# Turning the rows of the experts two tiles ahead in a four-layer metaformer

## What is computed

```
x = x + mixer_l(norm(x))            # l = 0: fractal, 1: involution, 2: splines, 3: squared-cosine attention
t = t + experts_l(norm(t))          # l = 0..3
# experts_l, for each token and each of its K chosen experts e:
h = act(x @ W1[e] + b1[e])          # layer 0: relu, top 1 of 8, F = 512, capacity, nan_to_num
y = weight * (h @ W2[e] + b2[e])    # layers 1, 2: gelu, top 2 of 8, F = 512 and 256
# layer 3, no biases: y = weight * ((silu(x @ W1[e]) * (x @ W2[e])) @ W3[e]), top 2 of 16, F = 256
```

## Time and profile before

| | |
|---|---|
| median of 3 runs | 2163.42 us (2162.23 to 2166.87) |
| profiled execution | 2167.0 us |
| its span, first to last instruction | 2165.2 us |
| mean granted clock of TensorE | 0.907 of full speed |
| TensorE, VectorE busy | 81%, 72% |

### The profile page before, as it was taken

One profiled execution on the slowest core, in us unless ns is written; L12 is line 12 of the kernel. 1 busy time (PEld: TensorE's weight loads), 2 busy tenths in 40 slices (PEclk: granted clock), 3 DMA queues, 4 the chain that ended last, 5 costly groups with the idle time before them and its releaser, 6 DMA issues. The chain is left out here.

```text
span 2165.2 us, 44747 instructions
## 1 busy us (share of the span) xinstructions
PE 1762.2 (81%) x10980; PEld 1383.6 (64%) x10981; DVE 1550.7 (72%) x4814; ACT 1200.6 (55%) x2719; POOL 957.5 (44%) x959
## 2 busy tenths in 40 slices
PE   2687666898588888899896776788859999979996
PEld 2233666897343434799895444667647777778996
DVE  8998887679677777655787576645866677665575
ACT  5455776798333323677685333556655444455664
POOL 0000234444105243675652277777630354557765
PEclk9999666999699999999998787798979999999998
DMA  3002002232201020132531112235422010124365
GB/s 81 0 0 78 18 24 61 60 94 84 87 5 36 22 61 29 56 97 77 151 102 50 56 51 80 70 99 155 138 77 98 20 37 31 54 54 105 100 196 157
DMA packets 183595, 154.30 MB, mean 71 GB/s; under 512 B 40294, under 2 KB 162822, under 8 KB 183362
## 3 DMA queue, kind: packets, MB, share of 16 engines
q1 hardware_dynamic: 153410, 92.37, 16.1%
q0 software_dynamic: 29952, 59.26, 8.1%
HBM read 85.33 MB, written 68.79 MB: 71 GB/s over the span
## 5 line engine op out<-in xcount | busy, mean ns | idle before, releaser
L1756 POOL DMA_INDIRECT returned<-rows_second_choice x488 | 495.9, 1016 | 310.2 <-DVE rows_second_choice L1677 107.4
L1307 POOL DMA_INDIRECT dispatched<-rows_first_choice,slot x192 | 191.9, 999 | 493.7 <-DVE rows_second_choice L1203 441.6
L1536 PE MATMUL psum<-rows_first_choice 128*128 128x128 f32 x2816 | 382.7, 280 | 19.4 <-DVE rows_first_choice L1658 19.2
L1536 PEld LDWEIGHTS psum<-rows_first_choice 128*128 128x128 f32 x2816 | 349.5, 195 | 24.5 <-DVE rows_first_choice L1658 23.5
L1546 PE MATMUL psum<-expert_weights,rows_first_choice 128*128 x2240 | 323.9, 283 | 24.6 <-DVE rows_second_choice L1674 11.0
L1546 PEld LDWEIGHTS psum<-expert_weights,rows_first_choice 128*128 128x128 f32 x2240 | 282.8, 195 | 37.5 <-issue 33.1
L1606 ACT ACTIVATE rows_first_choice<-psum,bias_columns 128x128 f32<-128x128 f32 x832 | 238.4, 375 | 91.3 <-PE psum L1536 89.2
L1307 POOL DMA_INDIRECT dispatched<-rows_second_choice,slot x192 | 187.9, 979 | 58.5 <-issue 58.2
L1307 POOL DMA_INDIRECT dispatched<-rows_first_choice,expert_weights x64 | 61.8, 966 | 266.7 <-DVE rows_first_choice L1201 249.4
L1589 ACT ACTIVATE rows_first_choice<-expert_weights 128x512 f32 x216 | 136.8, 634 | 44.0 <-issue 43.6
L1528 PE MATMUL psum<-identity,rows_second_choice 128*128 128x128 f32 x488 | 137.6, 283 | 14.1 <-DMA rows_second_choice<-dispatched 14.0
(11 more groups left out here) (423 smaller groups left out, 3834.1 us busy)
## 6 DMA issues: line engine op xcount, KB each, us to landing
rows_second_choice<-dispatched SPq DMA_DIRECT2D x488, 65.0 KB
rows_second_choice<-returned SPq DMA_DIRECT2D x10, 1024.0 KB, 6.0
returned<-rows_second_choice POOLq DMA_INDIRECT x488
expert_weights<-in_L_ffn_w SPq DMA_DIRECT2D x3, 2048.0 KB, 8.3
expert_weights<-returned SPq DMA_DIRECT2D x6, 1024.0 KB, 5.6
channel_major<-returned SPq DMA_DIRECT2D x6, 1024.0 KB, 7.1
residual<-in_x SPq DMA_DIRECT2D x8, 512.0 KB, 7.3
rows_second_choice<-returned SPq DMA_DIRECT2D x8, 512.0 KB, 4.4
```

The costliest lines, as they stand in the source:

```text
L1307: pool.indirect_dma_start(out=self.k.dispatched, out_offset=bass.IndirectOffsetOnAxis(ap=self.slot[:, b % 2, c, t:t + 1], axis=0), in_=sel ...
L1536: ins = pe.matmul(k.ps[:, self.PSH + u % 2, j * P:(j + 1) * P], self.wc[:, u % 2, j * P:(j + 1) * P], self.xt[:, u % 2, :], start=True, st ...
L1756: pool.indirect_dma_start(out=k.returned[0:N * self.K, :], out_offset=bass.IndirectOffsetOnAxis(ap=self.rt[:, u, C:C + 1].bitcast(I32), ax ...
```

## The change

Rows are turned two tiles ahead: in step t TensorE turns tile t+2 and VectorE copies tile t+2. Two turns and two copies stand ahead of the first step instead of one. The turned rows have four places instead of two. A turn now also waits until the copy of the tile two before it has read the PSUM bank. copy_rows waits in all layers until the hidden of four tiles before has read the place. The weight copies of VectorE raise `w_copied`, as ScalarE's did already, and hidden waits for it in all layers. Two more places of 128 columns shift rooms of the next norm in layer 2 by 256 columns.

```diff
-            rooms = [k.wts[:, 8192:8192 + 2 * IMG], rows1[:, late:late + 2 * IMG], rows0[:, 3840:3840 + 2 * IMG]]
-            slots = [rows0[:, 5888:5888 + IMG], rows0[:, 5888 + IMG:5888 + 2 * IMG], k.ch[:, N:N + IMG]]
+            rooms = [k.wts[:, 8192:8192 + 2 * IMG], rows1[:, late:late + 2 * IMG], rows0[:, 4096:4096 + 2 * IMG]]
+            slots = [rows0[:, 6144:6144 + IMG], rows0[:, 6144 + IMG:6144 + 2 * IMG], k.ch[:, N:N + IMG]]
...
-        self.xt, self.wc, self.hs = room(0, 2, C), room(0, 2, wide), room(0, self.HB, F)
+        self.xt, self.wc, self.hs = room(0, 4, C), room(0, 2, wide), room(0, self.HB, F)
...
         def turn_rows(t, u):
             pe.wait_ge(s_row[u].h, s_row[u].base + (t - u) * (16 // RING) + 16)
+            if past(t, 2):
+                pe.wait_ge(*self.when("x_copied", t - 1))
...
         def hidden(t, u):
             pe.wait_ge(*self.when("x_copied", t + 1))
-            if not self.vector_copies:
-                pe.wait_ge(*self.when("w_copied", t + 1))
+            pe.wait_ge(*self.when("w_copied", t + 1))
...
-                                self.xt[:, u % 2, :], start=True, stop=True)
+                                self.xt[:, u % 4, :], start=True, stop=True)
...
         def step(t, u, last):
             at = t if isinstance(t, int) else -1
-            if not last:
-                turn_rows(t + 1, (u + 1) % RING)
+            if not isinstance(t, int) or t + 2 < self.T:
+                turn_rows(t + 2, (u + 2) % RING)
...
         turn_rows(0, 0)
+        turn_rows(1, 1)
...
-            dve.tensor_copy(self.wc[:, u % 2, :], self.first[:, bass.ds(e, 1), :].rearrange("p a f -> p (a f)"))
+            dve.tensor_copy(self.wc[:, u % 2, :],
+                            self.first[:, bass.ds(e, 1), :].rearrange("p a f -> p (a f)")).then_inc(self.s["w_copied"].h, 1)
 
         def copy_rows(t, u):
             dve.wait_ge(*self.when("x_turned", t + 1))
-            if past(t, 2) and not self.vector_copies:
-                dve.wait_ge(*self.when("hidden_ready", t - 1))
-            dve.tensor_copy(self.xt[:, u % 2, :], k.ps[:, self.PSX + u % 2, 0:P]).then_inc(self.s["x_copied"].h, 1)
+            if past(t, 4):
+                dve.wait_ge(*self.when("hidden_ready", t - 3))
+            dve.tensor_copy(self.xt[:, u % 4, :], k.ps[:, self.PSX + u % 2, 0:P]).then_inc(self.s["x_copied"].h, 1)
...
-            if not last:
-                copy_rows(t + 1, (u + 1) % RING)
+            if not isinstance(t, int) or t + 2 < self.T:
+                copy_rows(t + 2, (u + 2) % RING)
...
         copy_rows(0, 0)
+        copy_rows(1, 1)
...
-        k.advance(x_turned=T, x_copied=T, w_copied=0 if self.vector_copies else T, hidden_ready=T, act_ready=T,
+        k.advance(x_turned=T, x_copied=T, w_copied=T, hidden_ready=T, act_ready=T,
```

## The result

| | before | changed |
|---|---|---|
| median, us | 2164.86 (2162.23 to 2166.87, 5 runs) | 2174.24 (2167.37 to 2178.46, 5 runs) |
| the same, measured a second time | 2165.59 (27 runs) | 2175.24 (2173.29 to 2176.24, 5 runs) |
| profiled execution, its span | 2167.0, 2165.2 | 2167.37, 2165.6 |

What follows compares the result with a forecast made beforehand. TensorE, busy 81%, was taken as the bound, its gaps waits for VectorE's copies and DMA rows. Terms 6.5 + 1.2 - 0.9 - 0.6 - 1.6 gave +4.6 us, median 2168.0; own range 2164.5 to 2171.5, 8-in-10 range 2157 to 2174.

Steps and rivals of the forecast that it cites:

- Late rows: Where DMA rows arrive without slack, a turn made earlier delays one more result and hidden: +6.5 us in all.
- row 24: Layer 0, at 427.50: first row needing every dispatch landed; TensorE held one step longer, +1.8 us.
- the rows to 90: Layer 2, late row at 1506.52, where GpSimd's transfers no longer cover the wait: +1.45 us.
- row 98: Layer 2, late row at 1522.03 inside VectorE's full stretch: one step longer, +1.85 us.
- Starts: Start of each layer: VectorE copies three tiles instead of two before the last image's routing; +0.3 each, +1.2 us.
- The copy asked for earlier: Hidden needs an older copy: -0.9 us in layer 0, -0.6 in layers 1 and 2, -1.6 at layer 3's end.
- VectorE's full stretches: 478 to 520 and 1508 to 1560: VectorE busy 40.68 of 42 and 46.56 of 52 us, so it sets the pace.
- Rival A: Faster: waits for copies in three stretches vanish because TensorE is really the pace; about -9 us, 2154; chance 0.15.
- Added waits: One more wait per turn, and in layers 1 and 2 per hidden and copy: no cost, up to 0.1 us a tile if uncovered.
- the -0.6 of layers 1 and 2: Hidden there waits for VectorE's weight-copy semaphore, raised one copy sooner: 0.2 to 0.3 us gained once per layer.
- three stretches: Where TensorE's waits for copies mostly lie: 6.1 us at 478 to 520, 6.1 at 1046 to 1080, 5.0 at 1508 to 1560.
- The sum: Whole kernel: 6.5 + 1.2 - 0.9 - 0.6 - 1.6 = +4.6 us, median 2168.0.

Runs made afterwards that it cites:

- lead_3: Changed kernel with turns and copies three tiles ahead instead of two, same four places; 2185.95 us, 1.0093 of the kernel before.
- late_rows: Changed kernel with the suspected tiles (24; 70 to 90; 88 to 90 and 98; 17 to 49) back to one tile ahead; 2170.54 us, 1.0029 of the kernel before.
- waits_only: Changed kernel without its order: four places, semaphore and added waits, but turns and copies one tile ahead; 2165.91 us, 1.0008 of the kernel before.
- before_apart: Kernel before, with layer 1's second and third 1 MB loads moved from tiles 88 and 89 to 90 and 91; 2166.57 us, ratio 1.0008.
- ends_03: Kernel before, with two tiles ahead only from tile 50 on in layer 0 and tile 88 on in layer 3; 2166.60 us, ratio 1.0013.
- ends_apart: Kernel before, two ahead only from tile 50 in layer 0 and 88 in layer 3, plus layer 1's two 1 MB loads put later; 2164.15 us, ratio 1.0000.
- lead_12: Kernel before, with two tiles ahead in layers 1 and 2 alone and the weight-copy semaphore; 2172.15 us, ratio 1.0029.

## Where the prediction held, and the step that failed

**Late rows: right at three places of four, and slightly too large.** Forecast 1.8 for row 24, 1.45 for the rows to 90, 1.85 for row 98, 1.4 for layer 3, 6.5 in all. Measured by the sends 1.4, 0.7 (its ranges overlap), 1.4 and 1.9 (1.3 of it by load to hidden): 5.4 us. At rows 24 and 98 the longer waits stand where they were foretold, grow with each tile further ahead (`lead_3`) and go back when the tile is put back (`late_rows`). For the rows to 90 no longer wait is seen, and the 1.45 is not shown.

**Starts: about right.** Forecast 0.3 a layer, 1.2; measured 0.7 in layer 1 and 0.3 in layer 0 (its ranges overlap), nothing to be told from the spread in the others. That the third copy is the cause was not tried.

**The copy asked for earlier: the right sign, too large in layer 3.** Forecast -0.9 at the end of layer 0 and -1.6 at that of layer 3; measured -0.7 and -0.8. Layer 0 shows why VectorE's full stretches give nothing more: 4.8 of 6.1 us of TensorE's waits came back at the turn and at the result behind it. Rival A fell on VectorE's 40.27 busy of 42 us.

**Added waits: right, with one tile ahead.** Nothing that could be told from zero (`waits_only`). In the changed order the turn's new wait does hold TensorE (6.3 us in all), in place of hidden's.

**The step that failed: the -0.6 of layers 1 and 2.** The prediction held only the first and the last of its three stretches against VectorE's busy time; the 6.1 us at 1046 to 1080 got no cause, and layer 1 was priced at one copy sooner, -0.3. But 4.3 of the 6.1 us are one wait, in which VectorE itself waits for GpSimd, which has just changed from sending rows to folding and can't begin. With two tiles ahead this lasted 1.9 us longer on the mean (10.2 against 8.4), and the runs with moved loads show that the 1 MB loads beside it are what lengthens it. The row said so in its last figure: 6.1 us in 4 waits, the longest 4.3. A wait that long is not a queue of copies, and its chain (TensorE for VectorE, VectorE for GpSimd, GpSimd for nothing that shows) had to be followed to its end. The price of -0.3 in layer 1 should have been +1.9. Of layer 2's -0.3 no more than -0.1 is seen (sends 112 to 120).

The Trainium skill, GPSIMD Engine Reference, section 2.1 Instruction dispatch, has the price that the trace shows without a name: the first call of a freshly loaded routine behind MODIFY_POOL_CONFIG pays about 6 us for loading it, and no instruction shows it. Here it was 6.9 us with little traffic beside it and up to 10.6 with much. That the idle time is this loading is what the Trainium skill says; no run here shows it.

**The sum.** 5.4 + 1.0 - 1.5 + 1.9 = +6.8 us from the terms (6.5 by the table, which leaves out layer 0's start), +8.3 with the stretches whose spread is as wide as their difference, and 9.4 to 9.7 by the clock. Most bounds of the terms held (0.7 for the rows to 90 is below its 0.9, 0.7 for the start of layer 1 above its 0.45); what the sum lacked was a term. Its own range, 2164.5 to 2171.5, is not what these bounds add up to, either: together they reach from -14.7 to +8.9 us. Some 3 us of the measured loss are in no term.

**What stays open.** Why the two-ahead order meets GpSimd's change at a worse time: in its profile the first load is issued 5.1 us ahead of that change (1027.94 to 1033.0) and in that of before 5.5 (1028.47 to 1034.0), and in all eleven profiles with the loads in place it is 5.3 to 5.8 us at one ahead and 4.7 to 5.2 at two or three; that this shift is enough was not tried. And why `before_apart`, whose stretch is shorter, is not faster over its runs. For `ends_03` and `ends_apart` the step that turns two tiles accounts for part of the same question.

## What to carry to other kernels

Asking for work earlier moves a wait, and moves it in the wrong direction wherever its input is the late one: list for each step that is moved ahead the places where its input arrives with no slack, and charge one step for each, times the tiles ahead. An engine that is full gives little by being asked earlier (0.7 us at the end of layer 0). A change of order in the middle of a run costs, too, where a step has to do two turns (1.1 us in `ends_03`, some 2.5 in `late_rows`). Follow every wait of several microseconds to the engine that ends its chain, before you decide that an order can't move it.

## What the runs showed of the hardware

- GpSimd's first TENSOR_TENSOR behind its sends started 6.9 us after MODIFY_POOL_CONFIG with 54 to 127 GB/s of DMA traffic beside it, 7.2 with 83, 8.5 with 324 and 10.1 with 356. In one more profile (`waits_only`) it was 7.4 with 331, so the rate over these 4 us is not all of it. The fold itself takes 2.33 us every time.
- A wait of TensorE of about 2 us cost it some 1.5 us more in some profiles than in others (hidden of tiles 10 to 18 of layer 1: 18.91 us in `lead_12`, 17.43 in the kernel before). GpSimd's sends of tiles 10 to 24 take 36.2 to 36.4 us in all, so none of it got through there. Busy time of 908 to 912 us in layer 1, behind such a wait at tile 13, in `lead_12` and then in the kernel before; the column behind POOL is the granted clock:

```profile
908.00:912.00 4.00, 4.00 (x22) 4.00 (x23) 2.41 (x8) 0.64 (x3) 3.08 (x4) 0.57 0.12 37
```
```profile
908.00:912.00 4.00, 4.00 (x36) 4.00 (x37) 2.75 (x10) 1.44 (x6) 3.09 (x4) 1.00 0.13 37
```

With the clock at its lower level (1.2 GHz) for most of these microseconds 22 matmuls get done instead of 36. It fell so in five of the fourteen profiles, all of them two or three ahead in layer 0 or 1, though not in two others of that kind; whether the order makes it likelier can't be told from so few.
